# Two orders exchanged inside the steps of a transformer pipeline: normed before division, q and k products before the turning

## The chip, the cores and the metric

The kernel runs on one core of a Trainium2 chip. Its engines are TensorE (PE in the profile, PEld for its weight loads), VectorE (DVE), ScalarE (ACT), GpSimd (POOL) and SyncE (SP, which issues the DMAs). The metric is the device time of one execution in microseconds; the median of the runs counts.

## The reference

Two batches of 2,048 tokens of 128 features pass through four residual blocks. The bulk of the time is `ffn`, two transformer layers, which comes twice with the same weights:

```python
x = x + attn_a(layernorm(x))                 # softmax(x x^T) x, 2 x 2048 tokens
x = x + ffn(layernorm(x))                    # 2 layers of the following
x = x + attn_b(layernorm(x))
x = x + ffn(layernorm(x))
...
def layer(x):                                # 8 heads of 64, windows of 64 tokens
    q, k, v = split(shift_token(x) @ wqkv)
    q, k = rotary_xpos(l2norm(q) * qs, l2norm(k) * ksc)
    x = x + local_attention(q, k, v) @ wo    # own window and the one before
    a, g = split(layernorm(shift_token(x)) @ w1 + b1)
    return x + (a * gelu(g)) @ w2 + b2
```

The two uses of `ffn` are the two passes of the kernel through the same code (stages 2 and 4), with `attn_b` as stage 3 between them.

## The kernel before, in words

The engines are programmed one by one: each has its own instruction list, written out by hand, and semaphores are the only tie between them. An engine works through its list in order; an instruction whose semaphore isn't there holds up all that stands behind it on the same engine. Nothing is planned by a tool.

A pass through the layers (`layers_pe`, `layers_act`, `layers_dve`, `layers_pool`, `layers_sp`) has 64 tiles of 128 tokens (32 for each layer) and 68 steps. It is a pipeline: in step s, tile s enters, and later parts of the tiles s-1 to s-4 are worked on:

- TensorE: `scores` and `take_off_maxima` of tile s-3 (L816 to L834), `turn_result` of tile s-4 (four transposes into bank 7, L860), `feed_bank_6` (feed-forward products into bank 6), `project` of tile s (q and k, six products of 512 columns into banks 0 and 1, L199 to L201), `values` of s-2, `feed_bank_7`, `project_out` of s-4 (L871), `maxima` of s-2 (L796, L801), `gather` of s-3 (attention weights times values into banks 6 and 7, L852).
- VectorE: `divide` of s-4 (reciprocal L1296 and product L1299 out of banks 6 and 7), `normed` of s-1 (L1260, reads banks 0 and 1, writes qn), `low` of s-2 (L1277), `rope` of s-1 (L1270, two SBUF inputs), gated products (L1323), `norms` of s (L1254), `scaled` (L1312), `add_second` (L1333), `add_out` of s-4 (L1305), `reduce_maxima` of s-2 (L1289).
- ScalarE: `high` and `high_there` of s-2 (L1072, L1079), `exps` of s-3 (L1093), `copy_result` of s-4 (L1098), `squares` of s (L1059), `copy_values` of s-2 (L1087), `rnorms` of s (L1064, L1066), and for the feed-forward part `gate` (L1137), `square`, `deviation` and `gelus`, which are framed by two loads of activation tables (L1143, L1196).
- GpSimd: the sine product of `rope` of s-1 (L1430, after `normed`), two additions into `ta` (L1436, after VectorE's `rope`), and splits for the feed-forward part.
- SyncE: rope tables, transposing DMAs of the split q and k (after `high` and after `low`), shifts of value rows, shifted copies of the stream.

The feed-forward layer goes by chunks of 512 tokens, one for four steps. `chunk_at(s, r)` is the chunk whose work with lag r falls in step s; it exists only where s - r is a multiple of four. So the steps differ by s modulo 4. The gelus of a chunk lie in the steps with remainder 0 (lag 12), and lag 13 falls in the step behind them.

The waits that touch the change are these: `project(s)` waits for `la_qn` (`normed(s-1)` has read banks 0 and 1); `normed(i)` waits for `la_rn` (`rnorms(i)` on ScalarE) and `la_tc` (GpSimd's sine product of the tile before); `turn_result(i)` and `feed_bank_6` wait for `la_ot` (`divide(i)`); `divide(i)` waits for `la_d` (`gather(i)` in the step before); `gather` waits for the readers of the feed-forward products in banks 6 and 7 (`fed_banks_free`); GpSimd's sine product waits for `la_qn`.

Of the kernel before, what the change touches and what calls it, by code (L numbers as in the profile page):

```python
# [50 lines left out]
def build(nc, a, out):  # L51
    ctx = ExitStack()
    with ctx:
# [561 lines left out]
        def chunk_at(s, r):  # L615

            C, rest = divmod(s - r, 4)
            return C if rest == 0 and 0 <= C < NC else None
# [122 lines left out]
        def layers_pe(e, stage, u, k):  # L741
# [25 lines left out]
            def project(i):  # L767
                l = tile(i)[0]
                ts = slice((i % 4) * 128, (i % 4) * 128 + 128)
                h, hl = attended(HH, i // 4)[:, ts], attended(HL, i // 4)[:, ts]  # L770
                e.wait_ge(S.sl_lo, NC * u + i // 4 + 1)
                e.wait_ge(S.la_qn, hi(i))
                for x in range(2):
                    xs = slice(x * 512, (x + 1) * 512)
                    mm = halves(e.e, PS[:, x, :], h, hl, wqh[:, l, xs], wql[:, l, xs])
                mm.then_inc(S.la_pj, 1)
# [53 lines left out]
            def take_off_maxima(i):  # L830
                e.wait_ge(S.la_mr, hi(i) + 1)
                for s in range(2):
                    for c in range(4):
                        mm = e.e.matmul(PS[:, 4 + s, 128 * c:128 * c + 128],  # L834
                                        BL.mx[i % 2][:, 4 * s + c:4 * s + c + 1].to_broadcast([128, 128]), idb[:, :],
                                        start=False, stop=True, skip_group_check=True)
                mm.then_inc(S.la_s, 1)
# [113 lines left out]
            for s in range(STEPS):  # L951
                on = lambda lag: 0 <= s - lag < TS
                if on(3):
                    scores(s - 3)
                    take_off_maxima(s - 3)
                if on(4):
                    turn_result(s - 4)
                feed_bank_6(s)
                if on(0):
                    project(s)  # L960
                if s == 0:
                    norm(range(7, NCH + 2))
                if on(2):
                    values(s - 2)
                feed_bank_7(s)
                if u == 0 and s == 1:
                    first_weights()
                late = chunk_at(s, 9) is not None
                if on(4) and not late:
                    project_out(s - 4)  # L970
                if on(2):
                    maxima(s - 2)
                if on(4) and late:
                    project_out(s - 4)
                if on(3):
                    gather(s - 3)
                if s == STEPS - 2 and u == 1:
                    e.wait_ge(S.la_mr, hi(TS - 1) + 1)
                    for g in range(4):
                        result(g, (2, 3, 0, 1)[g])  # L980
                if s == STEPS - 1:
                    if u == 1:
                        e.wait_ge(S.ou_cp, 2)
                    variance(NC - 1, 1)
# [58 lines left out]
        def layers_act(e, stage, u, k):  # L1043
# [3 lines left out]
            def norm(part):  # L1047
                layernorm_act(e, k, BM, part, BESIDE)
# [82 lines left out]
            def gate(C, i, bank):  # L1131
                n = 3 * (NP * u + C) + i
                wd, l = CW[i], C // NCH
                e.wait_ge(S.ff_g, n + 1)
                e.wait_ge(S.ff_hf, n - 3 + 1)
                e.wait_ge(S.w_bb, 1)
                e.e.activation(BF.gl[i][0:wd, :], PS[0:wd, bank, :], ACT.Identity,  # L1137
                               bias=b1r[0:wd, l, 3 + i:4 + i]).then_inc(S.ff_ev, 1)
# [24 lines left out]
            for s in range(STEPS):  # L1163
                on = lambda lag: 0 <= s - lag < TS
                if chunk_at(s, 11) is not None:
                    high_normed(chunk_at(s, 11))
                if on(2):
                    high(s - 2)
                if on(2):
                    high_there(s - 2)  # L1170
                if on(3):
                    exps(s - 3)
                if on(4):
                    copy_result(s - 4)
                if s == STEPS - 1:
                    if u == 1:
                        result(2, 0)
                    square(NC - 1, 4)
                if chunk_at(s, 12) is not None:
                    gate(chunk_at(s, 12), 2, 6)  # L1180
                if on(0):
                    squares(s)
                if s == 0:
                    norm(range(7, 8))
                if chunk_at(s, 9) is not None:
                    square(chunk_at(s, 9), 5)
                if chunk_at(s, 10) is not None:
                    deviation(chunk_at(s, 10), 6)
                if on(2):
                    copy_values(s - 2)  # L1190
                if chunk_at(s, 11) is not None:
                    gate(chunk_at(s, 11), 0, 6)
                    gate(chunk_at(s, 11), 1, 7)
                if chunk_at(s, 12) is not None:
                    gelus(chunk_at(s, 12), range(3))
                    e.e.preload_act_table_set("natural_log_exp_and_others")  # L1196
                if on(0):
                    rnorms(s)
                if s == 0:
                    norm(range(8, NCH + 2))  # L1200
                if u == 0 and s == 1:
                    first_weights()
                if chunk_at(s, -2):
                    high_for_attention(chunk_at(s, -2))
                if s == STEPS - 2:
                    high_for_feed_forward(NC - 1)
                    if u == 1:
                        result(0, 2)
# [21 lines left out]
        def layers_dve(e, stage, u, k):  # L1230
# [25 lines left out]
            def normed(i):  # L1256
                ss = BL.ss[:, i % 2, :]
                e.wait_ge(S.la_rn, 2 * hi(i) + 2)
                e.wait_ge(S.la_tc, hi(i - 1) + 1)
                e.e.scalar_tensor_tensor(BL.qn, ss[:, 16:32].rearrange("p (a o) -> p a o", o=1)  # L1260
                                         .to_broadcast([128, 2 * NH, DH]), 1e12,
                                         PS[:, 0:2, :].rearrange("p x (h d) -> p (x h) d", d=DH), ALU.min,
                                         ALU.mult).then_inc(S.la_qn, 1)
# [28 lines left out]
            def divide(i):  # L1292
                sums = PS[:, 6:8, 0:4 * (DH + 1)].rearrange("p b (h d) -> p b h d", d=DH + 1)
                rc = BL.rc[i % 2]
                e.wait_ge(S.la_d, hi(i) + 1)
                e.e.reciprocal(rc, sums[:, :, :, DH:DH + 1]).then_inc(S.la_rc, 1)  # L1296
                e.wait_ge(S.la_rc, hi(i) + 1)
                e.wait_ge(S.la_ox, hi(i))
                e.e.tensor_tensor(BL.o, sums[:, :, :, 0:DH], rc.to_broadcast([128, 2, 4, DH]), ALU.mult).then_inc(S.la_ot, 1)  # L1299
# [51 lines left out]

            for s in range(STEPS):
                on = lambda lag: 0 <= s - lag < TS
                if on(4):
                    divide(s - 4)
                if on(1):
                    normed(s - 1)
                if on(2):
                    low(s - 2)
                if on(1):  # L1360
                    rope(s - 1)
                if s == 1:
                    norm(range(6, NCH))
                if chunk_at(s, 13) is not None:
                    gated(chunk_at(s, 13), 0, 6)
                if on(0):
                    norms(s)
                if s == 0:
                    norm(range(5, 6))
                if chunk_at(s, 10) is not None:  # L1370
                    scaled(chunk_at(s, 10), 6)
                if chunk_at(s, 13) is not None:
                    gated(chunk_at(s, 13), 1, 7)
                if chunk_at(s, 14) is not None:
                    gated(chunk_at(s, 14), 2, 7)
                if chunk_at(s, 16) is not None:
                    add_second(chunk_at(s, 16), 7)
                if on(4):
                    add_out(s - 4)
                if u == 0 and s == 1:  # L1380
                    first_weights()
                if on(2):
                    reduce_maxima(s - 2)
                if u == 1 and s == STEPS - 2:
                    result(1, 3)
                    result(3, 1)
# [500 lines left out]
```

## Time and the profile before

| | us |
|---|---|
| median of 3 runs (lowest, highest) | 1581.75 (1580.46, 1586.36) |
| the profiled execution: device time | 1587.68 |
| its span in the trace | 1585.80 |
| busy in the span: TensorE, VectorE, ScalarE, GpSimd | 1431.8, 1356.6, 1227.6, 894.4 |

The granted TensorE clock is 0.977 of full speed over the span. A line of the timeline has the start in the span, the duration, the engine, the line of the kernel, the operation, output and inputs by name and shape, and how many neighbours were merged (x). In brackets stands how long the engine was idle before it and who ended that. The record of an instruction reaches some 0.07 us (VectorE) or 0.16 us (TensorE) into its successor's, so lengths in a queue are read from start to start.

### The profile page before, as it was taken

Reading aid. Unit: us, or ns where it says so; the run is one execution under the profiler, and the core shown is the slowest. Engines: PE = TensorE matmul, PEld = TensorE weight load, DVE = VectorE, ACT = ScalarE, POOL = GpSimd, SP = SyncE. Lnnn points to the kernel's source line nnn. Section 1 sums busy time; section 2 is a strip of 40 time slices with the busy share of each in tenths; the row PEclk is TensorE's granted clock in tenths of the full one; section 3 lists DMA queues with packets and bytes.
Section 4 is the critical chain, followed back from the end, with each engine's and each line's share of the span. In section 5 each row is a group of like instructions: output and inputs, shape, how many; then the busy total and the mean of one; then the engine's idle time right before and its main releaser. Section 6 shows DMA issues by size and latency. Waiting matters only on the chain.

```text
span 1585.8 us, 46462 instructions
## 1 busy us (share of the span) xinstructions
PE 1431.8 (90%) x18975; PEld 1120.9 (71%) x18975; DVE 1356.6 (86%) x1692; ACT 1227.6 (77%) x1834; POOL 894.4 (56%) x626
## 2 busy tenths in 40 slices
PE   5999997899999999999998757899999999999998
PEld 3777874777777777777776444677777777777776
DVE  6777757889999999999995866999999999999994
ACT  4876867678888888888885757688888888888884
POOL 3333005666666666676661645666666666766761
PEclk9999998999999999999999878999999999999999
DMA  4313003665665656657651003656656566665652
GB/s 120 107 47 97 4 7 72 126 120 118 114 125 121 121 115 123 121 116 122 128 96 28 0 7 69 128 123 120 121 123 120 118 120 123 119 122 122 115 103 73
DMA packets 359855, 157.46 MB, mean 99 GB/s; under 512 B 299410, under 2 KB 335836, under 8 KB 359644
## 3 DMA queue, kind: packets, MB, share of 16 engines
q1 hardware_dynamic: 359644, 154.51, 49.3%
q8 instruction: 150, 2.46, 0.7%
q14 instruction: 61, 0.50, 0.1%
HBM read 27.29 MB, written 6.29 MB: 21 GB/s over the span
## 4 chain that ended last, share of the span: by engine, by line
DVE 33%; ACT 23%; PE 19%; issue 11%; DMA 5%; POOL 5%; SPq 4%; DVEq 0%; ACTq 0%; POOLq 0%
DVE t L1270 9%; DMA t<-t 5%; POOL t L1436 4%; DVE t L1277 4%; DVE t L1289 4%; ACT t L1072 4%; DVE t L1254 3%; ACT t L1143 3%; PE PS L199 3%; PE PS L201 2%; DVE t L1323 2%; PE PS L200 2%; ACT t L1059 2%; ACT L1196 2%; ACT L1143 2%
## 5 line engine op out<-in xcount | busy, mean ns | idle before, releaser
L1430 POOL TENSOR_TENSOR t<-t 128x1024 f32<-128x1024 f32 x128 | 309.1, 2415 | 235.6 <-DVE t L1260 233.5
L1436 POOL TENSOR_TENSOR t<-t 128x512 f32<-128x512 f32 x256 | 319.5, 1270 | 147.8 <-DVE t L1270 147.5
L1270 DVE TENSOR_TENSOR t<-t 128x1024 f32<-128x1024 f32 x128 | 277.8, 2171 | 0.1
L1059 ACT ACTIVATE t<-PS 128x1024 f32<-128x1024 f32 x128 | 131.9, 1031 | 71.7 <-PE PS L201 71.6
L1277 DVE TENSOR_TENSOR t<-t,PS 128x1024 bf16<-128x1024 f32 x128 | 155.8, 1217 | 36.9 <-ACT PS L1079 36.9
L852 PE MATMUL PS<-t 128*64 128x65 f32 x4096 | 148.4, 225 | 41.9 <-DVE t L1323 40.0
L199 PE MATMUL PS<-wqh,HH 128*128 128x512 f32 x384 | 167.3, 436 | 18.6 <-DVE t L1260 16.0
L852 PEld LDWEIGHTS PS<-t 128*64 128x64 f32 x4096 | 130.6, 138 | 58.5 <-DVE t L1323 49.5
L1072 ACT CAST t<-t 128x1024 bf16<-128x1024 f32 x128 | 133.4, 1042 | 42.4 <-POOL t L1436 42.2
L1289 DVE TENSOR_REDUCE t<-PS 128x8 bf16<-128x1024 f32 x128 | 155.6, 1216 | 10.9 <-PE PS L801 10.9
L1254 DVE TENSOR_REDUCE t<-t 128x16 f32<-128x1024 f32 x128 | 154.3, 1206 | 7.5 <-ACT t L1059 7.4
L1093 ACT ACTIVATE t<-PS 128x1024 f32<-128x1024 f32 x128 | 130.9, 1023 | 36.9 <-PE PS L834 36.8
L1260 DVE SCALAR_TENSOR_TENSOR t<-t,PS 128x1024 f32<-128x1024 f32 x128 | 154.9, 1210 | 4.0 <-ACT t L1066 4.0
L201 PE MATMUL PS<-wqh,HL 128*128 128x512 f32 x384 | 152.4, 397 | 0.0
L200 PE MATMUL PS<-wql,HH 128*128 128x512 f32 x384 | 152.0, 396 | 0.0
L871 PEld LDWEIGHTS PS<-t,wo 128*128 128x128 f32 x1024 | 131.7, 191 | 22.1 <-issue 12.5
L1079 ACT CAST PS<-t 128x1024 f32<-128x1024 bf16 x128 | 130.2, 1017 | 15.0 <-DVE t L1289 4.7
L871 PE MATMUL PS<-t,wo 128*128 128x128 f32 x1024 | 138.0, 278 | 0.0
L827 PEld LDWEIGHTS PS<-t 64*128 64x128 bf16 x6144 | 109.0, 96 | 14.4 <-issue 0.5
L525 DVE TENSOR_TENSOR t<-t 128x1024 fp32r<-128x1024 f32 x64 | 80.1, 1258 | 39.3 <-ACT t L500 39.1
L827 PE MATMUL PS<-t 64*128 64x64 bf16 x6144 | 112.2, 191 | 0.0
L199 PEld LDWEIGHTS PS<-wqh,HH 128*128 128x128 f32 x384 | 73.1, 190 | 53.8 <-DVE t L1260 23.4
(242 smaller groups left out, 3389.6 us busy)
## 6 DMA issues: line engine op xcount, KB each, us to landing
t<-t SPq DMA_DIRECT2D x254, 130.0 KB, 2.3
t<-turns SPq DMA_DIRECT2D x128, 128.0 KB, 2.8
t<-yT SPq DMA_DIRECT2D x108, 128.0 KB, 2.3
t<-t SPq DMA_TRANSPOSE x304, 3.3
t<-in_c_rope SPq DMA_DIRECT2D x32, 128.0 KB, 2.2
turns<-t SPq DMA_DIRECT2D x32, 128.0 KB, 2.1
t<-in_L_attn_a_x SPq DMA_DIRECT2D x4, 512.0 KB, 6.7
t<-yT SPq DMA_DIRECT2D x16, 127.8 KB, 3.2
```

The costliest lines, as they stand in the source:

```text
L199: e.matmul(o, ah, bh, start=not more, stop=False, skip_group_check=True)
L201: return e.matmul(o, al, bh, start=False, stop=stop, skip_group_check=True)
L827: e.e.matmul(PS[:, 4 + s, 128 * c + 64 * w:128 * c + 64 * w + 64], kx[rows[s], 1, c, ks], qx[rows[s], 0, c, qs], start=False, stop=False, ...
L852: mm = e.e.matmul(PS[rows[w], 6 + h // 4, 65 * (h % 4):65 * (h % 4) + 65], BL.PT[i % 2][:, h % 2, qs], V[:, h, :], start=True, stop=True, ...
L871: mm = e.e.matmul(PS[:, 5, 0:128], wo[:, l, j, :], BL.ot[:, j, :], start=(j == 0), stop=(j == 3))
L1072: e.e.copy(BL.qh, BL.ta[i % 2].rearrange("p a b -> p (a b)")).then_inc(S.la_hi, 1)
L1254: e.e.tensor_reduce(ss[:, 0:16], BL.sq, AX.X, ALU.add).then_inc(S.la_ss, 1)
L1270: e.e.tensor_tensor(BL.ta[i % 2].rearrange("p (x h) d -> p x h d", x=2), BL.qn.rearrange("p (x h) d -> p x h d", x=2), cos.to_broadcast([1 ...
L1277: o = e.e.tensor_tensor(BL.ql, BL.ta[i % 2].rearrange("p a b -> p (a b)"), PS[:, 2:4, :].rearrange("p a b -> p (a b)"), ALU.subtract)
L1289: e.e.tensor_reduce(BL.mx[i % 2], PS[:, 2:4, :].rearrange("p s (c k) -> p (s c) k", k=128), AX.X, ALU.max, negate=True).then_inc(S.la_mr, 1)
L1430: e.e.tensor_tensor(BL.tc.rearrange("p (x h) d -> p x h d", x=2), BL.qn.rearrange("p (x h) d -> p x h d", x=2), sin.to_broadcast([128, 2, ...
L1436: e.e.tensor_tensor(tv[:, :, 32 * s:32 * s + 32], tv[:, :, 32 * s:32 * s + 32], BL.tc[:, :, 32 * (1 - s):32 * (1 - s) + 32], ALU.add).then ...
```

## The change

Three pieces of the order are exchanged; no instruction is added, removed or altered.

- TensorE: `project(s)` moves in front of `turn_result(s - 4)` and `feed_bank_6(s)`, in every step.
- ScalarE: the `gate` of lag 12 moves behind `squares(s)` (its product now comes behind `project` on TensorE).
- VectorE: `normed(s - 1)` moves in front of `divide(s - 4)`, but for the steps with a chunk of lag 13 (remainder 1), where the old order stays.

```diff
@@ layers_pe
                     take_off_maxima(s - 3)
+                if on(0):
+                    project(s)
                 if on(4):
                     turn_result(s - 4)
                 feed_bank_6(s)
-                if on(0):
-                    project(s)
@@ layers_act
-                if chunk_at(s, 12) is not None:
-                    gate(chunk_at(s, 12), 2, 6)
                 if on(0):
                     squares(s)
                 if s == 0:
                     norm(range(7, 8))
+                if chunk_at(s, 12) is not None:
+                    gate(chunk_at(s, 12), 2, 6)
@@ layers_dve
-                if on(4):
+                behind_gelus = chunk_at(s, 13) is not None
+                if on(4) and behind_gelus:
                     divide(s - 4)
                 if on(1):
                     normed(s - 1)
+                if on(4) and not behind_gelus:
+                    divide(s - 4)
                 if on(2):
                     low(s - 2)
```

## Rows read from the trace of the kernel before

**Rows 1.** The page, busy time of each engine.

```profile
PE 1431.8 (90%) x18975; PEld 1120.9 (71%) x18975; DVE 1356.6 (86%) x1692; ACT 1227.6 (77%) x1834; POOL 894.4 (56%) x626
```

**Rows 2.** Timeline of TensorE, one group of four steps, remainders 0 to 3.

```profile
1203.75 0.39 PE L816 MATMUL PS<-eye,mk 64*128 64x512 bf16 x2
...
1213.63 0.39 PE L816 MATMUL PS<-eye,mk 64*128 64x512 bf16 x2
...
1215.11 0.61 PE L860 MATMUL PS<-cst,t 128*128 128x128 f32 x4
1215.47 0.47 PE L199 MATMUL PS<-HH,w1h 128*114 128x512 f32 x1
...
1216.24 0.39 PE L199 MATMUL PS<-wqh,HH 128*128 128x512 f32 x1
...
1217.60 0.46 PE L199 MATMUL PS<-wqh,HH 128*128 128x512 f32 x1
...
1219.69 0.41 PE L796 MATMUL PS<-mk,eye 64*64 64x512 bf16 x4
...
1220.25 1.16 PE L871 MATMUL PS<-t,wo 128*128 128x128 f32 x8
1221.93 1.15 PE L852 MATMUL PS<-t 128*64 128x65 f32 x32 [0.53 <-DVE t L1323]
1223.02 0.39 PE L816 MATMUL PS<-eye,mk 64*128 64x512 bf16 x2
...
1231.19 1.15 PE L852 MATMUL PS<-t 128*64 128x65 f32 x32 [0.85 <-DVE t L1323]
1232.28 0.39 PE L816 MATMUL PS<-eye,mk 64*128 64x512 bf16 x2
...
1240.27 0.39 PE L816 MATMUL PS<-eye,mk 64*128 64x512 bf16 x2
```

**Rows 3.** Timeline of VectorE, the step with remainder 2.

```profile
1223.13 0.21 DVE L1296 RECIPROCAL t<-PS 128x8 f32<-128x8 f32 x1
...
1223.98 1.21 DVE L1260 SCALAR_TENSOR_TENSOR t<-t,PS 128x1024 f32<-128x1024 f32 x1
...
1226.24 2.50 DVE L1270 TENSOR_TENSOR t<-t 128x1024 f32<-128x1024 f32 x1
1228.67 1.20 DVE L1254 TENSOR_REDUCE t<-t 128x16 f32<-128x1024 f32 x1
...
1230.40 0.73 DVE L1323 SCALAR_TENSOR_TENSOR t<-PS,b1r,t 113x512 f32<-113x512 f32 x1
...
1232.39 0.21 DVE L1296 RECIPROCAL t<-PS 128x8 f32<-128x8 f32 x1
```

**Rows 4.** Timeline of GpSimd in the same step.

```profile
1225.28 2.39 POOL L1430 TENSOR_TENSOR t<-t 128x1024 f32<-128x1024 f32 x1 [3.27 <-DVE t L1260]
```

**Rows 5.** The page's groups: busy us, mean ns, idle before and its releaser.

```profile
L1270 DVE TENSOR_TENSOR t<-t 128x1024 f32<-128x1024 f32 x128 | 277.8, 2171 | 0.1
L1059 ACT ACTIVATE t<-PS 128x1024 f32<-128x1024 f32 x128 | 131.9, 1031 | 71.7 <-PE PS L201 71.6
```

**Rows 6.** Timeline of VectorE, the first tile of the second pass.

```profile
969.39 1.22 DVE L1270 TENSOR_TENSOR t<-t 128x1024 f32<-128x1024 f32 x1
```

**Rows 7.** Timeline of ScalarE, steps with remainders 0 and 1.

```profile
1207.11 0.58 ACT L1098 COPY t<-PS 128x512 f32<-128x512 f32 x1
...
1214.29 0.22 ACT L1066 ACTIVATE t<-t 128x16 f32<-128x16 f32 x1
```

**Rows 8.** Timeline of VectorE, the step with remainder 1.

```profile
1214.65 1.21 DVE L1260 SCALAR_TENSOR_TENSOR t<-t,PS 128x1024 f32<-128x1024 f32 x1
...
1221.80 0.27 DVE L1305 TENSOR_TENSOR yT<-PS,yT 128x128 f32<-128x128 f32 x1
```

**Rows 9.** Timeline of VectorE, two successive early steps of the second pass.

```profile
998.15 0.19 DVE L1296 RECIPROCAL t<-PS 128x8 f32<-128x8 f32 x1
...
1006.14 0.19 DVE L1296 RECIPROCAL t<-PS 128x8 f32<-128x8 f32 x1
```

## The prediction

> **What bounds the kernel now.** I read the page first: TensorE is called busy for 90% of the span and VectorE for 86% [rows 1], so the sums don't say which of them sets the time. The two passes through the layers fill about 1,200 us of it, and there the order within a step decides, so the next view is the timeline, engine by engine, over one group of four steps. I name the steps by s modulo 4: r0 holds the gelus and the second feed-forward product, r1 the centring and the first two gated products, r2 the variance and the third gated product, r3 the first two gate products.
>
> On TensorE a step begins with the mask product of `scores` (L816). The four lengths are 9.88, 9.39, 9.26 and 7.99 us, together 36.52 us [rows 2]. In r0 and r3 each product starts when the one before lets it: they are packed, and nothing can be won there by reordering. In r1 and r2 `gather` (L852) stands and waits for a gated product of VectorE, 0.53 and 0.85 us [rows 2]. So r2 is set by VectorE: from one reciprocal (L1296) to the next it works through 9.26 us without a pause [rows 3].
>
> In that row of work one instruction is too long: `rope`'s product (L1270) took 2.50 us in r2, 2,171 ns on the mean of 128, and 1.22 us where GpSimd had not begun its own rope product (L1430) [rows 3, 5, 6]. GpSimd's product ran from 1225.28 to 1227.67 and VectorE's ended at 1228.74, 1.07 us behind it [rows 3, 4]. So the end of `rope` on VectorE is: end of `normed` (L1260), 0.09 us, 2.39 us of GpSimd, 1.07 us. `normed` sets it, though on its own engine `low` (L1277) stands between.
>
> **The change part by part.**
>
> *VectorE, three steps of four: `normed` ahead of `divide`.* It removes and adds no instruction, and no moved piece issues a DMA or stands on the queue of SyncE or GpSimd. `divide` takes 0.85 us of the queue (1223.13 to 1223.98) [rows 3]. `normed` starts by so much earlier, GpSimd's product too, and `rope` on VectorE ends 0.85 us earlier; `low` stays where it is, since the two exchanged pieces are both ahead of it. This price goes by the row's fixed 1.07 us behind GpSimd's end, that is by one engine standing still for the other. Were it a slowing in proportion to the overlap, the excess of 1.28 us over 1.43 us of overlap [rows 3, 4, 6] would fall to 0.52 us over 0.58, a gain of 0.76. I take 0.85 and keep 0.76 as the lower end. The Trainium skill (SBUF — State Buffer, Who interferes with whom) says that a VectorE instruction with two SBUF inputs and a GpSimd instruction that reads SBUF exclude each other, and that the first to start holds on to the end: by it the gain is the 0.85, and the trace agrees, with its 1.07 us behind GpSimd's end. By the same page a `rope` that started first would hold GpSimd up instead; here `low` keeps it behind.
>
> *r2 in full, from VectorE's first instruction (zero).* `normed` is done at 1.21, TensorE's scores and maxima products are over at about 1.4 (in r1 from 1213.63 to 1215.11 with the wait for the division), so `project` (it waits for `normed` to have read its banks) starts at 1.4 at most, takes 1.36 (1216.24 to 1217.60) and the turning 0.36 (1215.11 to 1215.47) [rows 2]. On ScalarE the copy of the turned result starts at 3.3 and takes 0.46 to its successor, the squares some 1.05 more (a 128x1024 read of the kind of L1059, 1,031 ns on the mean [rows 5]): 4.8. `rope` is over for its queue at 5.54 - 0.85 = 4.69. So `norms` (L1254) starts at 4.8, not 5.54, 0.72 earlier, and `scaled`, `gated`, `gather` and the end of the step follow by 0.72. TensorE's own row in r2 has its 0.85 us wait to give, so it follows. r2 becomes 8.54 us. The low end is 0.5: the turned queries must land before maxima, and a DMA wait is there already now in some steps.
>
> *r3 and r0.* TensorE is packed in both, 7.99 and 9.88 us [rows 2], before and after; `rope`'s earlier end only makes slack. In r0 ScalarE's `copy_result` (L1098) now waits for a turning that stands behind `project`: turned at 1.42 + 1.36 + 0.36 and 0.2 for the pipeline, 3.4 after TensorE's start. It started at 1207.11, 3.36 after it, already [rows 2, 7]. `gate` behind `squares` is an exchange inside one uninterrupted row, so the gelus, two table loads and the inverse norms (L1066) come where they came, plus up to 0.1 us. Cost: 0 to 0.1.
>
> *r1: TensorE meets an unready `normed`.* L1066 ends at 1214.51 and `normed` runs 1214.65 to 1215.86, behind `divide` as before [rows 7, 8]. `project` was at 1216.24, behind turning and first product, and waited for nothing [rows 2]. Now it must start at 1215.86 + 0.1, while scores and maxima are over at 1215.1: 0.87 us of TensorE stand empty, and behind the waiting instruction stand the turning, the first product of `gated` 0, the values, the centring, maxima and output projection. From 1215.96: 1.36 for `project`, 0.36 for the turning, 0.77 for the first product (1215.47 to 1216.24), 1.83 from the values to maxima (1217.60 to 1219.69, less 0.26 for the pause ahead of maxima and for starting after a pause, my reading), 0.56 for maxima (1219.69 to 1220.25) and 1.16 for the output projection (L871): 1222.0 [rows 2]. `add_out` (L1305) started at 1221.80 [rows 8] and becomes 1222.1 to 1222.2, some 0.35 us later, with reduce-maxima and r2's `normed` behind it. The cover is the 0.5 us that TensorE stood before `gather` and VectorE's own row of work; gone with it would be the full 0.87. Bounds: 0.1 to 0.87, I take 0.37.
>
> *Sum for a group.* -0.72 + 0.37 = -0.35 us. Steps 14 to 65 are 13 groups in each pass (474.6 and 474.0 us in the trace, 36.5 a group): 26 x 0.35 = 9.1 us less.
>
> *Early steps.* Steps 4 to 13 lack most of the feed-forward work; there a plain step is 7.99 us [rows 9] and its loop is low, `rope`, GpSimd's two additions, `high`, `high_there`, low. `rope` ends by GpSimd there too, and gives back up to the 0.85. TensorE has 6.5 us of work in it (the r3 step's 7.99 without two first products of 0.7), so the loop can follow. Some are held by turned queries instead. I take 0.5 us for 8 of the steps in each pass: 8 us; bounds 0 and 13. Tail: 0 to 1; I take 0.5.
>
> In all 9.1 + 8 + 0.5 = 17.6 us. The profiled execution took 1587.68 us around a span of 1585.80; it is 0.4% above the median of the runs shown, 1581.75. 1587.68 becomes 1570.1; carried over to the median, **1564 us**.
>
> **The rivals.**
>
> *More is won (chance 0.17).* `add_out` in r1 doesn't come late, since the output projection's last product is through sooner than its 1.16 us, and VectorE's row decides everywhere but in the packed steps: -0.72 a group, 19 us, plus 8 to 13 in the early steps: 1551 us. For it speaks the 0.5 us wait of `gather` in r1 as cover, against it the single queue that now starts 0.87 late.
>
> *The chain moves to TensorE and DMA in r1 and r2 (0.18).* The empty 0.87 us pass on nearly in full, or the turned queries hold maxima back, and the gain of 0.72 is eaten; early steps give 3 to 6 us. 1577 us. That a change of order doesn't do anything, since the wait was only elsewhere, comes out at the same place.
>
> *Slower (0.1).* One mechanism: in r1 `project` waits for `normed`, and all behind it on TensorE; the point from which it decides is a delay of r2's start over 0.72 us. With 0.87 passed on in full, the copy in r0 another 0.2 late and r2's gain cut to 0.5 by the turned queries, a group is 0.57 longer: 15 us, less 4 from the early steps, 1593 us. For it speaks that r0's ScalarE chain and r1 hang on each other through L1066; against it that `gather` in r1 has 0.53 us of wait to give [rows 2].
>
> **How the numbers follow.** My forecast has 0.55, its own range 1557 to 1573 (26 x 0.2 to 0.5, early steps 4 to 11). What a measurement can tell from no change is 0.5%, 7.9 us: 1573.8 and 1589.7 are the borders. Faster: 0.55 x 0.97 + 0.17, and a little of the second case, 0.72. Same: 0.19. Slower: 0.09. The range leaves out part of the slow case and the best end of the first: 1549 to 1582.
>
> **What would show it.** L1270's mean falls from 2,171 to some 1,500 to 1,700 ns. GpSimd's L1430 starts behind L1260 as now, ahead of `divide`. Step lengths on TensorE: r2 near 8.5, r1 near 9.5 to 9.8, r0 and r3 unchanged. `project` in r1 waits about 0.9 us for L1260. ScalarE's L1098 waits for L860 in r0. If r0 or r3 shorten, I have called a step packed that wasn't; if r1 stays at 9.4, the first rival is right; if L1270 is not shorter, the whole account of `rope` is wrong.

## The result, and the profile after

The changed kernel takes 1587.0 us (median of 20 runs) against 1581.2 for the kernel before: a ratio of 1.0030, with the 95% interval [1.0020, 1.0041]. I had forecast 1564 us. The time lies outside my range and on the slow side, 0.3% above the kernel before, which is inside the 0.5% that I had set as the border of what can be told from no change.

The page of the changed kernel, busy time and three of its groups (columns as in [rows 5]):

```profile
PE 1449.5 (91%) x18975; PEld 1128.5 (71%) x18975; DVE 1299.9 (82%) x1692; ACT 1233.1 (78%) x1834; POOL 896.0 (56%) x626
...
L199 PE MATMUL PS<-wqh,HH 128*128 128x512 f32 x384 | 178.3, 464 | 34.6 <-DVE t L1260 33.3
L1270 DVE TENSOR_TENSOR t<-t 128x1024 f32<-128x1024 f32 x128 | 207.2, 1619 | 0.1
...
L1098 ACT COPY t<-PS 128x512 f32<-128x512 f32 x128 | 75.1, 587 | 102.8 <-PE PS L860 102.8
```

`rope` (L1270) fell from 2,171 to 1,619 ns [rows 5], and VectorE's busy time by 57 us [rows 1]. The time of the kernel didn't follow: TensorE's first product of `project` now waits 33 us in all for `normed` (L1260), 16 before, and ScalarE's copy of the turned result waits 103 us for the turning (L860), 5 before.

Where a group of four steps went, TensorE's row of the changed kernel, remainders 0 to 3 (to hold against [rows 2]):

```profile
1202.37 0.39 PE L816 MATMUL PS<-eye,mk 64*128 64x512 bf16 x2
...
1212.39 0.39 PE L816 MATMUL PS<-eye,mk 64*128 64x512 bf16 x2
...
1214.72 0.50 PE L199 MATMUL PS<-wqh,HH 128*128 128x512 f32 x1 [0.69 <-DVE t L1260]
...
1222.01 0.39 PE L816 MATMUL PS<-eye,mk 64*128 64x512 bf16 x2
...
1230.97 0.39 PE L816 MATMUL PS<-eye,mk 64*128 64x512 bf16 x2
...
1239.03 0.39 PE L816 MATMUL PS<-eye,mk 64*128 64x512 bf16 x2
```

The lengths are 10.02, 9.62, 8.96 and 8.06 us, 36.66 in all, where there were 9.88, 9.39, 9.26 and 7.99. The figures below are medians of such lengths over the steps 16 to 62 of both passes, from one start of L816 to the next. The labels are those of the runs of the next section; each ratio is taken against runs of the kernel before that were made together with it.

| kernel | r0 | r1 | r2 | r3 | group | ratio to before, 95% interval |
|---|---|---|---|---|---|---|
| before | 9.89 | 9.39 | 9.25 | 8.00 | 36.53 | 1 |
| changed | 10.02 | 9.64 | 8.96 | 8.07 | 36.69 | 1.0030 [1.0020, 1.0041] |
| old_order_r1 | 10.02 | 9.43 | 8.76 | 8.07 | 36.28 | 0.9945 [0.9926, 0.9963] |
| new_order_r2_only | 9.88 | 9.39 | 8.76 | 8.01 | 36.04 | 0.9906 [0.9890, 0.9922] |
| normed_first_always | 10.02 | 9.64 | 8.96 | 8.07 | 36.69 | 1.0017 [1.0002, 1.0032] |
| turning_in_two | 10.20 | 10.16 | 9.74 | 8.55 | 38.65 | one run, 1647.4 us |
| r2_squares_before_copy | 9.88 | 9.39 | 8.39 | 8.00 | 35.66 | 0.9851 [0.9835, 0.9867] |
| r2_only_early_old | 9.88 | 9.39 | 8.76 | 8.01 | 36.04 | 0.9940 [0.9926, 0.9953] |
| vectore_half_alone | 10.73 | 9.38 | 9.87 | 8.79 | 38.77 | one run, 1643.8 us |
| tensore_half_alone | 10.86 | 9.64 | 9.80 | 8.88 | 39.18 | one run, 1655.0 us |
| new_order_early_only | 9.88 | 9.39 | 9.25 | 8.00 | 36.52 | 0.9982 [0.9968, 0.9996] |
| changed_but_early | 10.03 | 9.64 | 8.96 | 8.08 | 36.71 | 1.0046 [1.0029, 1.0064] |
| squares_first_early_too | 9.88 | 9.38 | 8.40 | 8.00 | 35.66 | 0.9834 [0.9815, 0.9852] |
| before_again (control) | 9.88 | 9.39 | 9.25 | 8.01 | 36.53 | 0.9988 [0.9977, 0.9999] |

The control's interval misses 1 by a hair, so 0.1% more than an interval says is to be allowed for.

VectorE in r1 and the start of r2 of the changed kernel (to hold against [rows 8] and [rows 3]):

```profile
1213.45 1.22 DVE L1260 SCALAR_TENSOR_TENSOR t<-t,PS 128x1024 f32<-128x1024 f32 x1
...
1221.03 0.29 DVE L1305 TENSOR_TENSOR yT<-PS,yT 128x128 f32<-128x128 f32 x1 [0.35 <-PE PS L871]
...
1222.37 1.21 DVE L1260 SCALAR_TENSOR_TENSOR t<-t,PS 128x1024 f32<-128x1024 f32 x1
...
1225.47 1.66 DVE L1270 TENSOR_TENSOR t<-t 128x1024 f32<-128x1024 f32 x1
1227.31 1.22 DVE L1254 TENSOR_REDUCE t<-t 128x16 f32<-128x1024 f32 x1 [0.19 <-ACT t L1059]
...
1231.07 1.21 DVE L1260 SCALAR_TENSOR_TENSOR t<-t,PS 128x1024 f32<-128x1024 f32 x1
```

In r2 (1222.37 to 1231.07, 8.70 us) `rope` is short and leaves the queue early, but `norms` (L1254) now waits 0.19 us for the squares. In r1 `add_out` (L1305) waits for the output projection: it starts 7.58 us behind `normed`, where it was 7.15 [rows 8].

### The profile page after: what moved, and what is told of

Same layout as the page of the kernel before. It is cut to its first block, busy times and chain, and to the rows that moved or that the text cites. A ratio compares the mean times of both kernels' runs of the same rounds, so it can differ in the third digit from the quotient of the medians.

```text
span 1586.4 us, 46462 instructions
## 1 busy us (share of the span) xinstructions
PE 1449.5 (91%) x18975; PEld 1128.5 (71%) x18975; DVE 1299.9 (82%) x1692; ACT 1233.1 (78%) x1834; POOL 896.0 (56%) x626
## 4 chain that ended last, share of the span: by engine, by line
PE 56%; ACT 20%; DVE 11%; issue 6%; DMA 4%; SPq 3%; POOL 1%; DVEq 0%; POOLq 0%; ACTq 0%
PE PS L199 9%; PE PS L201 8%; PE PS L200 8%; PE PS L852 6%; PE PS L827 4%; PE PS L871 3%; PE PS L860 3%; DMA t<-t 3%; PE PS L834 3%; ACT t L1143 3%; ACT t L1059 2%; ACT L1196 2%; ACT L1143 2%; DVE t L1260 2%; PE PS L816 2%
## 5 line engine op out<-in xcount | busy, mean ns | idle before, releaser
L199 PE MATMUL PS<-wqh,HH 128*128 128x512 f32 x384 | 178.3, 464 | 34.6 <-DVE t L1260 33.3
L1270 DVE TENSOR_TENSOR t<-t 128x1024 f32<-128x1024 f32 x128 | 207.2, 1619 | 0.1
L1254 DVE TENSOR_REDUCE t<-t 128x16 f32<-128x1024 f32 x128 | 155.6, 1216 | 30.2 <-ACT t L1059 30.1
L1260 DVE SCALAR_TENSOR_TENSOR t<-t,PS 128x1024 f32<-128x1024 f32 x128 | 155.2, 1213 | 5.6 <-ACT t L1066 5.6
L1098 ACT COPY t<-PS 128x512 f32<-128x512 f32 x128 | 75.1, 587 | 102.8 <-PE PS L860 102.8
```

The lines of the kernel that those rows point to most:

```text
L199: e.matmul(o, ah, bh, start=not more, stop=False, skip_group_check=True)
L1270: e.e.tensor_tensor(BL.ta[i % 2].rearrange("p (x h) d -> p x h d", x=2), BL.qn.rearrange("p (x h) d -> p x h d", x=2), cos.to_broadcast([1 ...
```

## The experiments

**The old order on TensorE in r1.**

```diff
-                if on(0):
+                ahead = chunk_at(s, 13) is None
+                if on(0) and ahead:
                     project(s)
                 if on(4):
                     turn_result(s - 4)
                 feed_bank_6(s)
+                if on(0) and not ahead:
+                    project(s)
```

> The changed kernel, but in the steps with remainder 1 TensorE keeps the old order (turning and bank 6 ahead of project). Theory A, that r1 lost its time because project stands in front of everything while normed is unready: the wait of 0.87 us for L1260 goes, the first output addition comes again near 8.2 us after TensorE's start instead of 8.64, VectorE's r1 falls from 9.80 to about 9.35, r2 stays at its gain (8.70 on VectorE), r0 and r3 stay at 10.02 and 8.07 on TensorE. A group of four goes from 36.66 to about 36.2 us, 0.3 below the kernel before: ratio about 0.993. Theory B, that r1 is late for the pause ahead of maxima or for the output projection itself: r1 stays above 9.6 on VectorE and the ratio is 1.00 to 1.003.

Theory A held: r1 9.43, a group 36.28, ratio 0.9945. One kind of step of four, put back, turns a loss into a gain. (Step 13 is of this kind too; it is told apart below.)

**New orders in r2 only.** `ahead = s % 4 == 2 or s < 12` on TensorE, the same condition on VectorE, the old place of `gate` on ScalarE.

> New orders on TensorE and VectorE only in the steps with remainder 2 (and in the steps below 12, as in the changed kernel); everywhere else the orders of the kernel before, on ScalarE too. Theory A: r0 9.88, r1 about 9.35, r3 7.99 as before, r2 0.56 shorter on VectorE (8.70), a group near 36.0 us, ratio about 0.988 to 0.990. Theory C, that a second entry from bfloat16 or plain float32 products into the float32r ones costs TensorE 0.08 us a step and shows where it is packed: r0 and r3 lose their 0.14 and 0.07 again. Rival: r2's gain hangs on the new order in r3 or r0 (GpSimd's work comes earlier there), then the group stays above 36.3 and the ratio above 0.995.

r0 is 9.88 and r3 8.01 again, and r2 keeps its whole gain; ratio 0.9906. The packed steps had paid for an exchange from which they had nothing.

**No exception on VectorE.** `behind_gelus = False`.

> The changed kernel without the exception on VectorE: normed ahead of the division in r1 too. Theory A: normed there is held only by L1066, which ends 0.8 to 0.85 us after TensorE's start of the step, instead of starting at 1.06; project starts 0.2 us earlier, and the step that follows too: VectorE's r1 9.6 instead of 9.80, a group 36.45, ratio about 1.000 against the kernel before. Rival: the division comes late behind the waiting normed, and the turned result with it; then r1 is as long as with the exception or longer, ratio 1.003 or more.

The steps are those of the changed kernel (1.0017 [1.0002, 1.0032] beside 1.0030 [1.0020, 1.0041]), and my expectation of a shorter r1 was wrong. VectorE's row in r1 (TensorE started at 1211.65):

```profile
1212.69 1.22 DVE L1260 SCALAR_TENSOR_TENSOR t<-t,PS 128x1024 f32<-128x1024 f32 x1 [0.78 <-ACT t L1066]
```

`normed` starts 1.04 us after TensorE, as with the exception (1.06). The inverse norms come no earlier, so the exception costs nothing in r1 and gives nothing: the division fills a wait.

**The turning in two halves around the products into bank 6.**

```diff
...
                 if on(4):
-                    turn_result(s - 4)
+                    turn_result(s - 4, range(2))
                 feed_bank_6(s)
+                if on(4):
+                    turn_result(s - 4, range(2, 4))
```

> The changed kernel with the four transposes of the turned result split: two in front of the feed-forward products into bank 6, two behind. One more entry from plain float32 into float32r products in r0, r1 and r3. Theory C (each entry costs 0.08 us): the packed steps grow on TensorE, r0 from 10.02 to 10.10 or more and r3 from 8.07 to 8.15. Rival, that the 0.07 and 0.14 came from waiting and not from the entries: r3 stays at 8.07 or grows only by what the later copy of the result makes others wait, which would show as idle time with a releaser.

r3 grew by 0.48 us, for another reason than the one tested. TensorE in r3: the two halves of the turning, the values behind the second half, then the weights of the product that follows them:

```profile
1276.61 0.38 PE L860 MATMUL PS<-cst,t 128*128 128x128 f32 x2
...
1277.52 0.38 PE L860 MATMUL PS<-cst,t 128*128 128x128 f32 x2
1277.66 0.48 PE L199 MATMUL PS<-wqh,HH 128*128 128x512 f32 x1
1277.97 0.40 PE L200 MATMUL PS<-wql,HH 128*128 128x512 f32 x1
...
1278.58 0.17 PEld L199 LDWEIGHTS PS<-HH,w1h 128*114 128x114 f32 x1 [0.41 <-ACT t L1101]
```

The values do start with the slow 0.31 us of an entry. But the two halves of the turning take 0.13 and 0.14 us to their successors, where the four transposes in a row take 0.36, so the 0.08 us of the third entry are given back there. The step's 0.48 us lie in waits for ScalarE, first for its late copy (the 0.41 us above), then ahead of `gather`. As a test of theory C it is inconclusive.

**The squares ahead of the copy in r2.** On ScalarE, to new_order_r2_only:

```diff
+                early = s % 4 == 2
+                if on(0) and early:
+                    squares(s)
                 if on(4):
                     copy_result(s - 4)
...
-                if on(0):
+                if on(0) and not early:
                     squares(s)
```

> The kernel new_order_r2_only, and in r2 ScalarE also takes the squares ahead of the copy of the turned result. Theory A says that norms in r2 starts 0.2 us behind rope's end only because the copy stands waiting for the turning ahead of the squares: norms then starts right behind rope, the idle time in front of L1254 with releaser L1059 goes, VectorE's r2 falls from 8.75 to about 8.55 us, a group from 36.0 to 35.85, ratio about 0.989. Rival: the copy, now later by some 0.8 us, holds the third gated product's bank 7 and with it the gated product and gather; then r2 is 8.75 or longer and the ratio is 0.991 or more.

Better than expected: r2 8.39, ratio 0.9851. VectorE's r2 in this kernel (its `normed` is L1266, `rope` L1276, `norms` L1260):

```profile
1199.36 1.20 DVE L1266 SCALAR_TENSOR_TENSOR t<-t,PS 128x1024 f32<-128x1024 f32 x1
...
1202.45 1.67 DVE L1276 TENSOR_TENSOR t<-t 128x1024 f32<-128x1024 f32 x1
1204.05 1.21 DVE L1260 TENSOR_REDUCE t<-t 128x16 f32<-128x1024 f32 x1
...
1207.77 0.21 DVE L1302 RECIPROCAL t<-PS 128x8 f32<-128x8 f32 x1
```

`norms` starts 4.69 us after `normed`, without a wait; it was 5.54 us from the division in the kernel before [rows 3]. That is 0.85 us, the price that I had set on `divide` ahead of `normed`, in full, and VectorE's whole step is 8.41 us instead of 9.26.

**The early steps in the old order.** The condition of new_order_r2_only without `or s < 12`.

> The kernel new_order_r2_only with the old orders also in the steps below 12, so the early steps are new only where the remainder is 2. If the early steps brought 4 us in all (96.9 to 94.8 us a pass on the mean of the profiled runs), the ratio is 0.993 against 0.9906; if they brought 8 us, as I forecast, 0.996. The steps from 14 on are as in new_order_r2_only, a group of 36.0 us. Rival: the early steps are held by DMAs in either order, then the ratio is the same 0.991.

0.9940 against 0.9906 is 5 us, more than the new orders give in the early steps by themselves (below: 2.5 to 2.8). In the profiles steps 3 to 12 of both passes took 168.1 us here and 165.4 in new_order_r2_only, but 169.4 and 164.9 in the two profiles of the kernel before: one kernel scatters there by more than the difference. Whether orders that alternate from step to step cost something stays open.

**Each half alone.** VectorE's piece with TensorE and ScalarE in the old order; and TensorE's and ScalarE's pieces with the division always first.

> Only VectorE's piece of the change; TensorE and ScalarE keep the old orders. Theory A: the turning now waits on TensorE for a division 1.13 us later, some 0.6 us with nothing to do in r0, r2 and r3: r0 10.5, r3 8.6, r2 on VectorE 9.6 (the squares come later), r1 as before; a group about 38.1 us, 1.026 of the time before. rope is short all the same (mean near 1.6 us). Rival: rope's shortening pays for itself also without TensorE's piece; then a group is under 36.5.

> TensorE's and ScalarE's pieces of the change, with the division ahead of normed in every step on VectorE. Theory A: project waits some 0.85 us for L1260 in every step: r0 and r3 grow by 0.85 and the 0.08 of the second entry (10.8 and 8.9), r1 as in the changed kernel (9.8 on VectorE), r2 9.5; a group about 39.2 us, 1.04 of the time before. rope keeps its mean near 2.2 us. Rival: TensorE has enough slack, and a group is not over 37.

Groups of 38.77 and 39.18 us: each half makes r0 and r3 0.8 to 1.0 us longer, and TensorE then waits for the other half. In the first that wait is 0.64 us in r0 and 0.57 in r3 (medians), as I had priced it, but the steps grew by 0.85 and 0.79; I didn't follow up the 0.2 us between. Neither half pays by itself. ScalarE's piece was not run alone.

**What the early steps give.** New orders below step 12 alone; and the changed kernel with the old orders there.

> New orders only in the steps below 12 of each pass, the orders of the kernel before in all others. Theory D, that the early steps gave 4 us in all (193.4 to 189.6 in the profiled runs, steps 3 to 13 of both passes): ratio 0.9975. My forecast of 8 us: 0.995. Rival: the kernel before had a bad draw of DMA waits in its profiled execution and the early steps give under 2 us: ratio 0.999 to 1.000. The steps from 14 on: a group of 36.5 us, as before.

> The changed kernel with the old orders in the steps below 12. Theory A and C with the medians of the steps from 16 on: a group 0.14 us longer than before, 26 groups 3.6 us, ratio 1.0023, and the early steps as before. Then the changed kernel's own 1.003 holds no gain from the early steps. If the early steps do give 4 us to the changed kernel, this one lies at 1.0055.

0.9982, and 1.0046 against 1.0030 with the new orders there: the early steps give 2.8 us by the first run (interval 0.6 to 5.1) and 2.5 by the second, whose interval overlaps with that of the changed kernel. The changed steps behind them cost 7.3 us, where 26 groups of 0.16 us explain 4.2. Most of the rest is one step of each pass, told below.

**The squares first in the early steps too.** `early = s % 4 == 2 or s < 12`.

> The kernel r2_squares_before_copy, with the squares ahead of the copy also in the steps below 12. Theory A: where project stands in front of the turning, the copy's wait keeps ScalarE from the squares by 0.5 us in those steps too; up to 0.3 us for 8 steps in each pass, 3 to 5 us: ratio 0.982 to 0.983. Rival: the early steps are held by the chain from rope over GpSimd's additions to the transposing DMAs, not by norms: ratio 0.985, as without it.

0.9834 beside 0.9851, the two intervals overlap: 1557.3 us is the best median here, but this last step is not told from none.

**Control.**

> The kernel before, unchanged, as a control: ratio 1.000 with 1 inside its interval. Its second profile tells how far the parts that the change can't touch scatter: the stretch ahead of the first step (266.2 us) and the early steps (193.4 us for both passes). If the early steps come at 190 or less here, the 193.4 was a draw and not the kernel.

Steps 3 to 13 came at 188.4 us and the stretch ahead of the first step at 262.8, where the first profile had 193.4 and 266.2. That stretch, which the change can't touch, lies between 259.8 and 267.2 us over the profiles of this study. One profile doesn't settle 5 us outside the regular groups.

## Why the prediction was wrong

*`normed` ahead of `divide`, 0.85 us off `rope`.* Right: L1270's mean fell to 1,619 ns, and in r2_squares_before_copy the whole 0.85 us shows. In r2 of the changed kernel GpSimd's product ended at 1226.05 and `rope` at 1227.13:

```profile
1223.66 2.39 POOL L1433 TENSOR_TENSOR t<-t 128x1024 f32<-128x1024 f32 x1 [2.82 <-DVE t L1260]
```

That is 1.08 us behind, the same distance with an overlap of 0.58 us instead of 1.43. In the steps 14 to 65 of both kernels and both passes the median is 1.08 us in each of the four kinds, with overlaps up to 1.44. So it was standing still and not slowing in proportion; with the rule of the Trainium skill that I had weighed (SBUF — State Buffer, Who interferes with whom) the trace agrees.

*r2, -0.72.* Right mechanism, mis-sized: -0.56 on VectorE (9.26 to 8.70). I had the squares as the second limit at 4.8 (which is 0.74 before 5.54, not 0.72); they came at 4.94. `project` began 0.14 us earlier than I took, at 1.26, and took 0.14 longer, 1.50 us and not 1.36 (1223.63 to 1225.13); the rest is the copy, which started at 3.39 instead of 3.3, and some 0.05 us behind it. r2_squares_before_copy, where the squares don't wait for the copy, gives the 0.85 in full.

*r3 and r0 "packed ... cost 0 to 0.1".* They were packed, so everything added counts, and the sum had nothing for it. Something was added: 0.07 us in r3 and 0.13 in r0. TensorE's row of the changed kernel in r3, `project` and the first product behind the turning:

```profile
1232.42 0.48 PE L199 MATMUL PS<-wqh,HH 128*128 128x512 f32 x1
1232.73 0.40 PE L200 MATMUL PS<-wql,HH 128*128 128x512 f32 x1
1232.97 0.39 PE L201 MATMUL PS<-wqh,HL 128*128 128x512 f32 x1
...
1233.88 0.60 PE L860 MATMUL PS<-cst,t 128*128 128x128 f32 x4
1234.23 0.47 PE L199 MATMUL PS<-HH,w1h 128*114 128x512 f32 x1
1234.55 0.40 PE L200 MATMUL PS<-HL,w1h 128*114 128x512 f32 x1
1234.78 0.40 PE L201 MATMUL PS<-HH,w1l 128*114 128x512 f32 x1
```

The first product takes 0.31 or 0.32 us to its successor, the others 0.23. Over the steps 16 to 62 of the second pass the median is 0.31 behind L834 (35 without a wait between) and behind L860 (35), and 0.23 behind another float32r product (105). The old order had one such entry ahead of the values (L834, L860, then nine products in a row), the new one has two. That is 0.08 us a step; r0 has 0.06 more, since `project` starts 1.53 us after the step there and 1.45 in r3, right behind the end of `normed` (1203.75 in the group shown, `project` at 1203.90). The cause is shown as far as r0 and r3 lose it with the old order; what in the entry takes the time, the type or the weight load, stays open, and turning_in_two didn't settle it: its third entry took 0.31 too, but the divided turning gave that back and the late copy of the result covered the sum.

*r1, +0.37.* Right mechanism, and mis-sized by 0.13: it was +0.50 on VectorE (9.32 to 9.82). `project` started 2.33 us after the step, as forecast; then it took 1.50 us and not 1.36, 0.11 of that in its first product (0.34 instead of 0.23), and the row from the values to the maxima took 1.93 where I had 1.83. old_order_r1 puts the step back to 9.37. My cover, the 0.5 us that TensorE stood before `gather`, was no cover: `gather` did lose its wait, but `add_out` stands behind the output projection on VectorE and starts the next step's `normed`.

*Sum for a group, -0.35.* It was +0.16: -0.29 in r2 as TensorE's starts have it, +0.25 in r1, +0.13 in r0, +0.07 in r3. Each of the three costs was taken some 0.1 us too small and the gain 0.16 too large, and 26 groups multiplied that: 4.2 us instead of -9.1. (The two stretches that I gave as 474.6 and 474.0 us are 474.9 and 473.2 from TensorE's starts; nothing hangs on it.)

*Early steps, 8 us.* 2.5 to 2.8 us. I had counted 0.5 us for 16 steps from one pair of rows [rows 9]; which of them are held by something else no run settles.

*Not seen at all: step 13.* It follows the first gelus. Step 12 has no second feed-forward product, so TensorE arrives early and ScalarE late. Before, the turning and a product stood ahead of `project`; now nothing does. TensorE of the changed kernel, the wait and some of the products behind it; then windows (window, length, PE, PEld, DVE, ACT, POOL busy, granted clock, DMA share, GB/s):

```profile
1065.67 0.50 PE L199 MATMUL PS<-wqh,HH 128*128 128x512 f32 x1 [3.27 <-DVE t L1260]
...
1069.48 0.63 PE L199 MATMUL PS<-wqh,HH 128*128 128x512 f32 x1
1069.90 0.60 PE L200 MATMUL PS<-wql,HH 128*128 128x512 f32 x1
1070.33 0.41 PE L201 MATMUL PS<-wqh,HL 128*128 128x512 f32 x1
```

```profile
1060.00:1065.60 5.60, 2.41 (x88) 1.99 (x82) 3.05 (x4) 5.44 (x9) 2.69 (x3) 1.00 0.31 74
1065.60:1068.00 2.40, 2.33 (x10) 1.91 (x11) 1.58 (x3) 1.76 (x2) 2.30 (x1) 0.78 0.59 115
1068.00:1070.50 2.50, 2.50 (x8) 1.99 (x8) 1.94 (x3) 1.51 (x2) 1.34 (x3) 0.53 0.66 125
1070.50:1074.00 3.50, 3.50 (x52) 2.62 (x52) 2.26 (x4) 2.43 (x5) 1.28 (x2) 1.00 0.28 56
```

TensorE stood 3.27 us, and behind that its granted clock was 0.53 in a window of 2.5 us, about the 1.2 GHz level, and products there took 0.42 us to their successors and not 0.23. In the first pass it stood 3.15 us, and the clock was 0.50 from 354.0 to 356.5. Before, the wait for L1260 in this step was 1.57 and 1.56 us, and the clock stayed at 1.00. Step 13 took 13.44 and 13.80 us in the two passes, where the two profiles of the kernel before have 11.06 to 12.50 (mean 11.89): 3.5 us for both passes together. old_order_r1 has 11.46 and 12.28 and the full clock, though its steps ahead are new: the order on TensorE is the cause. How much of it is the idle time and how much the clock is not separated. The row from 1066.93 to 1070.33 took 3.40 us and would take 1.8 at full speed, an estimate from the 0.23 and 0.31 us of the products and the 0.36 of the turning; these 1.6 us are about the whole lengthening. But in vectore_half_alone the clock fell in this step too, and it took only 12.28 and 12.38 us.

Together: 26 x 0.16 = 4.2, plus 3.5, less 2.8 for the early steps is +4.9 us, where 0.0030 of 1581.2 is 4.7 [3.2, 6.5]. The same sum gives 26 x -0.25 - 2.8 = -9.3 for old_order_r1 (measured -8.7), 26 x -0.49 - 2.8 = -15.5 for new_order_r2_only (-14.9) and 26 x -0.87 - 2.8 = -25.4 for r2_squares_before_copy (-23.6 [-21.0, -26.1]). By the medians the account holds within the intervals; only r2_only_early_old lies 3 us beside it. But the agreement of the first sum is in part luck. The steps 14 to 65 of both passes together took 950.7, 951.0 and 951.1 us in the three profiles with the new order on TensorE there (the changed kernel, normed_first_always, changed_but_early), and 948.1, 949.4 and 948.7 in the three with the old orders there (before, before_again, new_order_early_only). That is 2.2 us more and not 4.2: a median leaves out the steps that are longer or shorter than their kind. With 2.2 the sum is +2.9 us, so some 2 us of the loss stay open. The slower rival (1593 us) lies nearest in time and names r1. Its point of decision, 0.72 us of delay there, was not reached; by TensorE's starts r2 gained 0.29 us, of which r0 and r3 took 0.20, so 0.09 us of delay in r1 were enough, and there were 0.25. The rival in which the chain moves to TensorE (1577 us) had the place right too, but not a loss.

**Which steps of the prediction failed.** From the 17.6 us that I had added up to the 4.7 us lost are 22.3. By the medians, 26 groups miss 4.2 us by the gain in r2 (0.56 instead of 0.72), 5.2 by r0 and r3 (0.20 where the sum had nothing) and 3.4 by r1 (0.50 instead of 0.37). The early steps miss 5.2 (2.8 instead of 8), step 13, which had no term, 3.5, and the tail 0.5, for which no profile shows a gain (35.6 us behind the last step's start before and after). The mechanism at `rope` was right; the costs that the exchange brought to the other kinds of step, and the gain in the early steps, were not.

## What to carry to other kernels

An exchange of order has to be judged step kind by step kind: it pays only in the kind whose bound it shortens, and in a kind where an engine is packed every small cost that it brings counts whole. Before a producer's consumer is moved to the front of an in-order queue, look in each kind of step, the first odd ones too, at when the producer is ready; what stood ahead of it was filling that wait. When the new critical instruction waits for something that a third engine keeps behind other work, move that as well: the squares ahead of the copy were worth 0.5% on top of 0.9% (0.9851 and 0.9906).

## What the runs showed of the hardware that I had not expected

- The first float32r product of 512 columns behind the bfloat16 products of L834 or the plain float32 transposes of L860 takes 0.31 us to its successor, 0.23 in a row of its kind. Behind the plain float32 product of 512 columns in r2 (L907) it takes 0.63, in both orders.
- A pause of 3.3 us on TensorE was followed by a window with a granted clock of 0.53; behind the pauses of 0.69 us in r1 and 0.45 us in r2 it stayed at 1.00. Between them the length of the pause alone doesn't tell: in step 13 of vectore_half_alone the clock fell behind a pause of 1.76 us (one of 0.64 us stood 10 us ahead), and behind one of 1.90 us in old_order_r1 it stayed at 1.00.
- `rope` on VectorE ended 1.08 us behind the end of GpSimd's product, whether the two overlapped by 0.58 or by 1.43 us; alone it took 1.22.
